# A selective scan between two FFNs: the sum over the 16 states as accumulating transposes instead of fp32 products with an identity

## The reference, cut to what matters

```
def step(h, inp):                        # h: batch x 512 x 16, 2048 steps
    dA_t, dB_t, x_t, C_t, t = inp
    h = h * dA_t + dB_t * x_t[:, :, None]
    nrm = jnp.sqrt(jnp.sum(h * h, axis=(1, 2), keepdims=True))
    fac = jnp.minimum(20.0 / (nrm + 1e-08), 1.0)
    h = jnp.where(t % 10 == 0, h * fac, h)
    y = jnp.einsum('bdn,bn->bd', h, C_t) + D_param * x_t
    return (h, y)
```

## Time and profile before

| | |
|---|---|
| median of three runs | 1543.17 us (1541.73 to 1543.39) |
| profiled execution, its span | 1540.7 us, 25357 instructions |
| PE busy / PEld busy | 1463.5 us (95%) / 1017.9 us (66%) |
| DVE busy | 1256.0 us (82%) |
| ACT busy | 1122.5 us (73%) |
| POOL busy | 934.8 us (61%) |
| L1343, the scan on DVE | x820, 882 ns each |
| L1167, the sum over states on PE | x1664 MATMULs, 439 ns mean, 525.7 us |

### The profile page before, as it was taken

How to read it: one execution, slowest core, us unless ns; L and a number is a source line. 1 busy time by engine, 2 the same in 40 slices (tenths; PEclk the granted TensorE clock), 3 DMA queues, 4 the chain that set the end, 5 groups by cost and what they waited for, 6 DMA issues and landing times.

```text
span 1540.7 us, 25357 instructions
## 1 busy us (share of the span) xinstructions
PE 1463.5 (95%) x6854; PEld 1017.9 (66%) x6854; DVE 1256.0 (82%) x2526; ACT 1122.5 (73%) x2618; POOL 934.8 (61%) x956
## 2 busy tenths in 40 slices
PE   6999999999989999999999999999999998999998
PEld 5555555555456777777777777777666665677776
DVE  7775566646468999999999999999999998788885
ACT  4454455445999999999999999999999964233243
POOL 0223313321359999999999999999999997400000
PEclk9999999999999999999999999999999999999999
DMA  8225437443757666656656666565544448466420
GB/s 268 82 64 161 133 98 208 129 146 109 241 147 204 177 165 179 172 162 184 170 154 185 172 169 184 156 174 167 139 110 109 99 102 227 119 210 198 147 86 28
DMA packets 231429, 236.27 MB, mean 153 GB/s; under 512 B 45913, under 2 KB 197145, under 8 KB 231289
## 3 DMA queue, kind: packets, MB, share of 16 engines
q1 hardware_dynamic: 230344, 233.34, 53.3%
q10 hardware_dynamic: 944, 1.31, 0.2%
HBM read 136.31 MB, written 98.56 MB: 152 GB/s over the span
## 4 chain that ended last, share of the span: by engine, by line
DVE 35%; POOL 13%; PE 11%; issue 6%; DMA 2%; DVEq 1%; POOLq 1%; SPq 0%; ACT 0%; ACTq 0%
DVE h L1343 22%; POOL rc L1107 13%; DVE banks L1333 8%; PE banks L1492 3%; PE banks L1513 3%; PE banks L1523 3%; DVE qs L1327 2%; DVEq L1341 1%; PE banks L1167 1%; DMA ub<-scratch_ub 1%; DMA q_xc<-scratch_xc 1%; DVE q_ln_st L1769 1%; DVE q_g L1678 1%; POOLq L1115 1%; DVE q_x L1650 1%
## 5 line engine op out<-in xcount | busy, mean ns | idle before, releaser
L1343 DVE TENSOR_TENSOR_SCAN h<-decay,banks 128x352 f32<-128x352 f32 x820 | 710.4, 882 | 57.6 <-DVE banks L1333 2.9
L1118 POOL TENSOR_TENSOR hc<-h,bc 128x640 f32<-128x640 f32 x410 | 592.7, 1446 | 0.0
L1167 PE MATMUL banks<-hc,w_ident 128*128 128x320 f32 (+1 forms) x1664 | 525.7, 439 | 0.1
L1236 ACT ACTIVATE tb<-dtc,a 128x320 f32<-128x320 f32 (+1 forms) x832 | 417.4, 556 | 4.8 <-DVE x L610 4.8
L1167 PEld LDWEIGHTS banks<-hc,w_ident 128*128 128x128 f32 x1664 | 284.4, 191 | 70.3 <-issue 0.4
L1258 ACT ACTIVATE decay<-tb 128x640 f32<-128x640 f32 x410 | 295.1, 723 | 0.0
L1107 POOL TENSOR_TENSOR rc<-qs,w_mhalf 128x1 f32<-128x1 f32 x410 | 224.9, 549 | 111.0 <-DVE qs L1327 111.0
L1153 PE MATMUL banks<-ub 128*128 128x176 f32 x1640 | 273.0, 289 | 2.9 <-DMA ub<-scratch_ub 2.9
L1146 PEld LDWEIGHTS banks<-sc_ss,sc_ones 128*128 128x128 f32 x820 | 123.2, 189 | 158.5 <-ACT sc_sq L1247 153.1
L1153 PEld LDWEIGHTS banks<-ub 128*128 128x128 f32 x1640 | 217.1, 193 | 3.1 <-DMA ub<-scratch_ub 3.0
L1146 PE MATMUL banks<-sc_ss,sc_ones 128*128 128x1 f32 x820 | 151.6, 254 | 37.8 <-ACT sc_sq L1247 20.3
(11 more groups left out here) (133 smaller groups left out, 1764.9 us busy)
## 6 DMA issues: line engine op xcount, KB each, us to landing
ub<-scratch_ub SPq DMA_DIRECT2D x410, 107.5 KB
bc<-scratch_blk SPq DMA_DIRECT2D x205, 160.0 KB, 3.5
scratch_ub<-turned SPq DMA_DIRECT2D x64, 512.0 KB, 3.8
scratch_ub<-spread SPq DMA_DIRECT2D x64, 176.0 KB, 3.0
scratch_xc<-xc SPq DMA_DIRECT2D x8, 1024.0 KB, 4.8
scratch_sg<-sg SPq DMA_DIRECT2D x8, 1024.0 KB, 5.9
piece<-scratch_u SPq DMA_DIRECT2D x32, 256.0 KB, 3.8
q_ys<-scratch_y SPq DMA_DIRECT2D x8, 1024.0 KB, 5.7
```

Source lines behind the costliest of these rows:

```text
L1118: pool.tensor_tensor(hc[:, pl % 2, :, at * S:(at + 1) * S] .rearrange("p (c b n) e -> p c b n e", c=KE, b=B)[:, :, b], state(m)[:, :, 0:S] ...
L1167: mm = pe.matmul(banks[:, y_bank(p), 0:KE * B * wide], w.ident[:], rhs, start=(n == 0), stop=(n == N - 1))
L1236: act.activation(tanh_rows(c, r), dtc[:, c % 2, k * B:(k + 1) * B, 0:blocks_of(c) * S].rearrange("p b (k e) -> p k b e", e=S), ACT.Tanh, s ...
L1343: dve.tensor_tensor_scan(state(m).rearrange("p r e -> p (r e)")[:, half], decay[:, m % DRING, half], psI[m % B][:, half], 0.0, ALU.mult, A ...
```

## The change

Sixteen time steps form a group: 16 steps by 8 pairs of chunk and batch are 128 columns. For each state n PE now transposes the 128 partitions by 128 columns of `hc` (a matmul with `is_transpose`), and the 16 transposes of a group add up in PSUM, so that the sum stands there turned: (step, pair) on the partitions, channels along the columns. There are 128 groups, so 2048 transposes, five per unit from unit 5 on. Four groups fill a bank. ACT copies the bank to `yt` in two halves (`copy_yt`), PE turns the four 128 x 128 squares back (`turn_back`), and ACT copies the result to `yc` in two halves, reading PSUM with a stride of 8 elements and writing time contiguously (`copy_y`). There are 32 such quads. `hc` becomes one ring of 80 steps with the 8 pairs innermost, so POOL's `weigh` writes with a stride of 8 elements from step to step where it wrote contiguous rows of ten. The projection of the first tile moves from the last six units to the last three and behind them. SP stores y in 16 chunks of 128 steps.

```diff
--- before.py
+++ after.py
@@ sizes
-QB = 4
-QUADS = (NB - 1) // QB + 1
-CQ = CB // QB
+GT = 16
+RT = math.lcm(S, GT)
+GROUPS = L // GT
+PAIRS = GROUPS // 2
+PT = 2 * GT
+QUADS = PAIRS // 2
+CP = 4
+YCHUNKS = PAIRS // CP
+TURNS = 5
+FILL = 320
+LAG = 5
...
+def blocks_in(g):
+    return (g * GT + GT - 1) // S + 1
+def summed_at(q):
+    return LAG + (4 * N * (q + 1) - 1) // TURNS
+def y_bank(q):
+    return 5 if q % 2 else 2
@@ buffers
-    hc = second.put("hc", [P, 2, ROWS, QB * S])
+    hc = second.put("hc", [P, N, RT, KE * B])
-    yc = second.put("yc", [P, 2, KE * B, CT])
+    yc = second.put("yc", [P, 2, KE * B, CP * PT])
+    yt = second.put("yt", [P, 4, P])
@@ SyncE
-                store_y(y_at[j], CQ)
+                store_y(y_at[j])
...
-        for c in range(len(y_at), last):
-            store_y(c, CQ)
-        store_y(last, QUADS - last * CQ)
+        for c in range(len(y_at), YCHUNKS):
+            store_y(c)
@@ GpSimd, weigh
-            if b == 0 and at == 0 and pl >= 2:
-                pool.wait_ge(y_summed, pl - 1)
+            if b == 0 and j * S >= RT:
+                pool.wait_ge(y_summed, (j * S + S - 1 - RT) // GT + 1)
             pool.tensor_tensor(
-                hc[:, pl % 2, :, at * S:(at + 1) * S]
-                .rearrange("p (c b n) e -> p c b n e", c=KE, b=B)[:, :, b],
+                hc[:, :, at:at + S, b::B].rearrange("p n t c -> p c n t"),
@@ TensorE
-        def readout(p, n0, n1):
...
-                mm = pe.matmul(banks[:, y_bank(p), 0:KE * B * wide], w.ident[:], rhs,
-                               start=(n == 0), stop=(n == N - 1))
+        def sum_turned(k0, k1):
+            for k in range(k0, min(k1, GROUPS * N)):
+                g, n = divmod(k, N)
+                if n == 0:
+                    pe.wait_ge(hc_ready, blocks_in(g) * B)
+                    if g % 4 == 0 and g >= 8:
+                        pe.wait_ge(y_copied, g // 2 - 2)
+                lhs = hc[:, n, g * GT % RT:g * GT % RT + GT, :].rearrange("p t r -> p (t r)")
+                mm = pe.matmul(psG[y_bank(g // 4)][:, g % 4, :], lhs, w.ident[:], is_transpose=True, start=(n == 0), stop=(n == N - 1))
+                if n == N - 1:
+                    mm.then_inc(y_summed, 1)
+        def turn_back(q):
+            pe.wait_ge(yt_copied, 2 * q + 2)
+            for x in range(4):
+                mm = pe.transpose(psG[y_bank(q)][:, x, :], yt[:, x, :], w.ident[:])
+            mm.then_inc(y_turned, 1)
+        def project_first(x0, x1):
+            for x in range(x0, x1):
+                if x == 0:
+                    pe.wait_ge(ut_lo, halves(PIECES))
+                    pe.wait_ge(y_copied, PAIRS - 2)
+                post.project(pe, 0, x // 2, x % 2 * KE // 2, (x % 2 + 1) * KE // 2)
...
-            if m >= UNITS - 6:
-                q, k = (m - UNITS + 6) // 2, (m - UNITS + 6) % 2 * (KE // 2)
...
-            if p >= 0:
-                readout(p, part * each, (part + 1) * each)
-            if m < QB * B + B:
+            if m >= UNITS - 3:
+                project_first((m - UNITS + 3) * 2, (m - UNITS + 4) * 2)
+            if m >= LAG:
+                sum_turned((m - LAG) * TURNS, (m - LAG + 1) * TURNS)
+            if m in backs:
+                turn_back(backs[m])
+            if m < 2 * LAG:
                 keep_busy(2 if m < B else 1)
...
-        readout(QUADS - 1, 0, N)
+        sum_turned((UNITS - LAG) * TURNS, (GROUPS - 1) * N)
+        project_first(6, 2 * G)
+        sum_turned((GROUPS - 1) * N, GROUPS * N)
+        turn_back(QUADS - 1)
@@ ScalarE
+        def copy_yt(q):
+            act.wait_ge(y_summed, 2 * q + 2 if q % 2 else 2 * q + 4)
...
+            act.activation(yt[:, half, :], psG[y_bank(q // 2)][:, half, :], ACT.Copy).then_inc(yt_copied, 1)
...
-            act.wait_ge(y_summed, p + 1)
-            act.activation(yc[:, c % 2, :, o:o + wide],
-                           banks[:, y_bank(p), 0:KE * B * wide].rearrange("p (c t) -> p c t", t=wide),
+            act.wait_ge(y_turned, q // 2 + 1)
+            act.activation(yc[:, c % 2, :, o:o + PT], psY[y_bank(q // 2)][:, q % 2 * PT:(q % 2 + 1) * PT, :].rearrange("p t r -> p r t"),
                            ACT.Copy).then_inc(y_copied, 1)
...
-            if p >= 0 and late == (1 if p <= LAST_EVEN else 0):
-                copy_y(p)
+            if m in sums:
+                copy_yt(sums[m])
+            if m in turns:
+                copy_y(turns[m])
```

More of the change, by code:

```diff
@@ L722 @@
 ROW = E + N * W
-LAST_EVEN = (UNITS - 6 - B) // (QB * B) - 2
-assert LAST_EVEN % 2 == 0 and (NB - 1) % QB == 0
+assert L % (CP * PT) == 0 and TT % (CP * PT) == 0
 Scan = namedtuple("Scan", """sync gpsimd tensor scalar vector load_first load_units tanhs decay_rates decay_scale masks
@@ L751, in halves @@
     return k if k < B else 2 * k - B
-def quad_of(j):
-    return (0, 0) if j == 0 else ((j - 1) // QB + 1, (j - 1) % QB)
-def quad_blocks(p):
-    return 1 if p == 0 else QB
-def quad_start(p):
-    return 0 if p == 0 else (p - 1) * QB + 1
-def y_bank(p):
-    if p == QUADS - 1:
-        return 4
-    return 2 if p % B == 0 and p <= LAST_EVEN else 5
-def y_before(p):
-    return p - 2 if p <= LAST_EVEN + 1 else p - 1
+def blocks_in(g):
[4 more added lines that the diff above has]
+    return 5 if q % 2 else 2
+assert all(LAG + N * g // TURNS >= blocks_in(g) * B for g in range(GROUPS))
 def scan_stage(nc, dram, w, areas, banks, sem, pre):
@@ L821, in scan_stage @@
     psT, psQ = banks[:, 3], banks[:, 4]
+    psY = {q: banks[:, q].rearrange("p (t r) -> p t r", r=KE * B) for q in (2, 5)}
+    psG = {q: banks[:, q].rearrange("p (g d) -> p g d", d=P) for q in (2, 5)}
     a_in, s_in, blk_out, consts = sem("a_in"), sem("s_in"), sem("blk_out"), sem("s_consts")
@@ L1033, in sync, with store_y @@
     def sync(sp, pre, post):
-        def store_y(c, quads):
-            t0 = quad_start(c * CQ) * S
-            wide = sum(quad_blocks(c * CQ + q) for q in range(quads)) * S
-            sp.wait_ge(y_copied, c * CQ + quads)
-            sp.dma_start(dram["y"][:, :, t0:t0 + wide], yc[:, c % 2, :, 0:wide]).then_inc(y_out[c % 2], 16)
+        def store_y(c):
+            sp.wait_ge(y_copied, (c + 1) * CP)
+            sp.dma_start(dram["y"][:, :, c * CP * PT:(c + 1) * CP * PT], yc[:, c % 2]).then_inc(y_out[c % 2], 16)
         QP = piece_unit(B + 1) // B
@@ L1053, in sync @@
             dt_at[free(x0 + 1, 1)] = (c, 1)
-        for c in range(CHUNKS):
-            if c * CB + CB + QB + 2 < NB:
-                x0 = free(c * CB + CB + QB + 2, 2)
+        for c in range(YCHUNKS):
+            at = summed_at(2 * c + 1) // B + 4
+            if at + 2 * QP < NB:
+                x0 = free(at, 2)
                 y_at[x0 + QP if x0 in dt_at else x0] = c
@@ L1172, in keep_busy @@
         def keep_busy(times):
             for _ in range(times):
-                pe.matmul(banks[:, 5, 0:KE * B * QB * S], w.ident[:], w.s1[:, 0, 0:KE * B * QB * S].bitcast(F32),
-                          start=True, stop=True)
+                pe.matmul(banks[:, 5, 0:FILL], w.ident[:], w.s1[:, 0, 0:FILL].bitcast(F32), start=True, stop=True)
         pieces = {piece_unit(k): k for k in range(B, PIECES)}
-        each = N // (QB * B)
+        backs = {summed_at(q) + 3: q for q in range(QUADS)}
@@ L1295, in scalar @@
         pieces = {piece_unit(k): k for k in range(B, PIECES)}
+        sums = {summed_at(q // 2) + 1 + q % 2: q for q in range(PAIRS - 2)}
+        turns = {summed_at(q // 2) + 4 + q % 2: q for q in range(PAIRS - 2)}
         for m in range(AHEAD):
@@ L1319, in scalar @@
                     copy_low(act, pieces[m - 8 - x], psT, x * E // 2, (x + 1) * E // 2)
-        for p in range(QUADS - 2, QUADS):
-            copy_y(p)
+        for x in range(2):
+            copy_yt(PAIRS - 2 + x)
+        for x in range(2):
+            copy_y(PAIRS - 2 + x)
     def vector(dve, pre, post):
@@ L1543, in tensor @@
         turn_xn(0)
-        pe.wait_ge(scan.y_copied, QUADS)
+        pe.wait_ge(scan.y_copied, PAIRS)
         up(0, 0, 1)
```

39 lines of the change are left out of this document (12 added, 27 removed).

## The result

The changed kernel takes 1581.04 us as median of four runs (1576.18 to 1587.70), the kernel before 1542.45 beside it: 1.025 times as long, 95% interval 1.022 to 1.029. The profiled execution has a span of 1583.1 us, 42.4 more than before. The prediction said 1577 (1539 to 1650).

A forecast was written before the change was run, and what follows sets the result against it. The loop of carry, scan, clamp and norm, 2.14 us, bounds the unit, with DVE's own work as long. Terms 0 + 2 + 0 + 32 - 1 = 33; 1540.7 + 33 + 2.5 = 1576, said as 1577 us, range 1539 to 1650.

The forecast's parts named there:

- The bound: Steady scan at full clock: PE's gain of 0.6 us per unit is worth 0 us, since the loop hides it.
- The sign that DVE's clamp would wait for PE: Scan at low clock: scans 2.3 to 2.8 us apart instead of 2.13, with DVE's clamp waiting for PE.
- The clock, 32 us: Scan: thinner PE work lets the clock fall repeatedly; low a quarter of the time, 0.6 of 55 us; bounds 0 and 220.
- ACT, 2 us: Units with pieces: added copies collide with piece copies and make ACT's squares late; 2 us, bounds 0 and 8.
- the strided read, nothing: ACT's copy back from PSUM with a stride: nothing extra; at worst twice its 364 ns.
- POOL, nothing, with a risk: POOL's weigh, writing steps 32 bytes apart instead of 4: 0 us taken, bounds 0 and 520.
- rival D: POOL's weigh pays for its stride, from 0.18 us on; a quarter more gives 75 us, 1618 us; chance 0.13.
- The tail, -1 us: End of the scan: turn_xn goes 0.4 us earlier and 0.6 is counted behind it; -1 us, bounds -3 and +1.5.
- A: Rival, scan: the clock holds, leaving 2 - 1; 1544 us; chance 0.18.
- B: Rival, last stage and first and last units: PE's relief makes it faster by 3 + 1; 1539 us; chance 0.11.
- C: Rival: the clock stays down for most of the scan, three quarters at full price; 1709 us; chance 0.08.
- E: Rival, scan: the 16-step groups are late, so weigh waits for its ring; given no chance of its own.

The follow-up runs named there:

- E1: The changed kernel with one more fp32 product of 176 columns ahead of the inputs of every unit from 12 to 403: 1554.14 us, ratio 1.0076.
- E2: The changed kernel with three added transposes of 128 columns per unit, result overwritten by the inputs: 1550.24 us, ratio 1.0062.
- E4: The kernel before with products of the state sum cut from 320 to 160 columns, first and last group excepted: 1590.30 us, ratio 1.0326.
- E10: The changed kernel with early projection and the sum's copies kept apart from piece copies, without an added product: 1575.15 us, ratio 1.0214.
- E6: The changed kernel with an added 288-column product and ACT's copies of the sum cut to 32 of 256 columns: 1550.83 us, ratio 1.0048.
- E8: The changed kernel with an added 288-column product, early projection and the sum's copies kept apart from piece copies: 1546.94 us, ratio 1.0028.
- E9: E8 with the added product at 176 columns, more products in the first units and products around turn_xn: 1539.34 us, ratio 0.9989.

## Why the prediction was right

**The bound.** PE's relief in a unit of 2.13 us is worth 0: held. Units at full clock take what they took, and E1 and E2, which give PE work back, lose nothing by it where no pieces run (175.3 and 175.2 us against 175.2). The sign that DVE's clamp would wait for PE came only where pieces run; without them it is `carry` that waits, for `inputs`.

**The clock, 32 us.** The mechanism held, and E1, E2 and E4 show it as the cause. Its size was too small. The low share was put at a quarter and was 35%; the low unit was put at 2.77 us with pieces and 2.36 without (2.43 with `turn_back`) and took 2.56 to 2.73 and 2.33 to 2.34, by the two ways of sorting. I took six tenths of the price, since each stretch would first use up PE's idle time (0.6 of 55 is 33, where the sum has 32; it comes to 1576 or 1577). Of the 42.7 us in units that saw a low clock, 30.7 are in the part with pieces, where it was low for 163 us, and 12.0 in the part without, low for 125. At the prediction's own full price these would be 163/2.77 x 0.64 = 38 and 125/2.43 x 0.30 = 15, together 53 us. So the discount was wrong: the price was paid to eight tenths in both parts, not six. That the quarter did no harm is luck: the full price came to 53 us instead of the 55 put down for it, because the greater share fell more on the cheap units without pieces. The quarter itself was a choice between 0 and 220 us, with no row behind it, so the mechanism was foreseen and the 4 us between 1577 and 1581 are not its merit. One picture behind the term was wrong too: that the clock comes back once PE is crowded at the low clock. Among pieces no low stretch lasted over 10.2 us, but from 1207.8 us it stayed at 0.50 for 64.9 us in which PE was busy all of the time:

```profile
1207.80:1272.60 64.80, 64.80 (x312) 64.53 (x313) 56.63 (x110) 56.68 (x147) 53.78 (x55) 0.50 0.41 92
```

**ACT, 2 us, and the strided read, nothing.** Held in the changed kernel: 364 and 362 ns, and units with pieces at full clock 2.152 instead of 2.144 us, which is 2.3 us over 286; with the copies apart and no product (E10) they take 2.145. But it holds only while PE has time to catch up. With PE filled again the same copies cost 5 to 7 us (E6, E8), above the 2 that I had counted for it.

**POOL, nothing, with a risk; rival D.** `weigh` took 1461 ns instead of 1446. That is 1% more for the strided write, and its 15 ns are under the 0.18 us that the loop leaves. D falls.

**The tail, -1 us.** It was +0.9. Up to `turn_xn` the working held: the residual came 6.6 us behind the end of the scan (7 was forecast), the last y copy was done 2.5 us ahead of `turn_xn`, and `turn_xn` started 13.0 us behind the end of the scan instead of 13.5, the half microsecond gained that was forecast. What failed lies behind it, where 0.6 less was counted and 1.4 more was spent: PE stood idle for 3.23 us ahead of `turn_xn`, the clock fell at 1381.9 for 6.8 us, and `turn_xn` took 1.97 us instead of 1.04, `up` behind it starting at the low clock too. The prediction gave that gap no price. In E9, with products in the gaps, `turn_xn` takes 1.09 us, and the stage from its start on is 2.1 us shorter than in the changed kernel.

**The rivals.** A (the clock holds, 1544) fell by the page. B (the relief is worth something) fell for this kernel; in E9 the tail wins 4.9 us, of which the relief's part isn't shown. C (the clock down for three quarters, 1709) fell: it was low for 35% of the scan. Nor is it the transposes as such that let it fall: between 500 and 1280 us E2, with transposes in the sum and as the added work, read 0.99 to 1.00, and E4, which has no transposes in its sum, 0.65 to 0.86. In E2 three fp32 transposes per unit kept the clock as well as the product did in E1, which read 0.99 to 1.00 too. E (the ring late) shows nowhere.

## What to carry to other kernels

Before taking work off a matmul engine that isn't the bound, ask what its work holds up: here 0.6 us less of PE per unit bought nothing, and with it gone the clock fell to 0.50 for 35% of the scan, and while it was low the products that PE makes for the loop came 0.214 us apart instead of 0.113. Here the cheaper form needed filler (28 us between E8 and E10), and it can pay only where PE is itself waited for, as at the end of a stage. Try the filler before judging the form: one line moved this kernel by 27 us. And price a copy that is added to a nearly full engine by the unit in which it lands, not by its mean.

## What the runs showed of the hardware

- Less work was slower: with half of the sum's columns left out the kernel before went from 1542 to 1590 us (E4).
- In the changed kernel, from 1207.8 us on, a TensorE that was busy for 64.80 of 64.8 us at a granted clock of 0.50 was not granted the full one in that time. There busy time at the low clock did not by itself bring the full one back. In E4 such stretches ended after 20 and 27 us, with PE busy for 27.20 of 27.30 us in one of them.
- Transposes of 128 columns in fp32 follow each other 0.109 us apart at full clock and 0.213 at the low one, and in the changed kernel 16 of them add up in PSUM for each group of 16 steps; `weigh` with a write stride of 32 bytes took 1461 ns for 640 elements per partition against 1446; ACT's read of PSUM with a stride of 8 elements took 364 ns for 256 columns against 362.
